# A decoder layer's state-space scan: half of the drives made by TensorE, three of four weighings on GpSimd, even and odd steps in turns

## What is computed

```python
u = conv(x) + conv_b                                   # causal, 4 taps, per channel
x_dbl = u @ xproj_w.T ; dt, Bm, Cm = split(x_dbl, 128 | 16 | 16)
delta = softplus(dt @ dtproj_w.T + dtproj_b)           # [b, token, channel]
deltaA = exp(delta[..., None] * A)                     # A = -exp(A_log): 16 states a channel
deltaBu = delta[..., None] * Bm[:, :, None, :] * u[..., None]
h = dA * h + dBu ; y = sum_n h[n] * c[n]               # for every token, in order
y = y + u * D_skip
```

## Time and profile before

| | us |
|---|---|
| median of 3 runs | 239.72 (239.43 to 240.22) |
| the profiled execution's own time | 240.53 |
| its span, first to last instruction | 238.7 |
| first scan starts | 29.98 |
| last scan ends | 168.7 |
| busy: VectorE, ScalarE, TensorE, GpSimd | 207.0, 155.1, 153.4, 151.4 |

### The profile page before, as it was taken

The page is one execution under the profiler, slowest core; times in us unless marked ns, Lnnn a source line. Parts: engine busy times, 40 slices in busy tenths (PEclk is TensorE's granted clock), DMA queues, the critical chain, the costliest instruction groups (busy, mean ns, idle before and its releaser), DMA issues.

```text
span 238.7 us, 3180 instructions
## 1 busy us (share of the span) xinstructions
PE 153.4 (64%) x804; PEld 115.0 (48%) x804; DVE 207.0 (87%) x436; ACT 155.1 (65%) x332; POOL 151.4 (63%) x166
## 2 busy tenths in 40 slices
PE   0169780987735857776495566575966776756554
PEld 0136470865724556674394545453944453533141
DVE  2297999989899899999999999999999998983841
ACT  2155889883798866857796677486357796843240
POOL 3410497498868498979888987697417354550732
PEclk9999998599795555958679997786797999995667
DMA  6992822753633445645463324310000000100003
GB/s 166 308 357 86 221 93 76 188 138 100 194 93 93 137 122 136 131 105 141 105 162 113 131 50 138 86 39 1 4 0 0 0 0 3 45 0 0 0 0 132
DMA packets 15105, 23.25 MB, mean 97 GB/s; under 512 B 1136, under 2 KB 6640, under 8 KB 15088
## 3 DMA queue, kind: packets, MB, share of 16 engines
q1 hardware_dynamic: 13792, 21.92, 33.2%
q10 hardware_dynamic: 1296, 1.15, 1.4%
HBM read 21.88 MB, written 1.18 MB: 97 GB/s over the span
## 4 chain that ended last, share of the span: by engine, by line
DVE 34%; PE 26%; issue 18%; ACT 13%; POOL 3%; DMA 2%; SPq 1%; DVEq 0%; POOLq 0%; ACTq 0%
DVE hid L1063 9%; DVE prod L1074 6%; PE pY L750 6%; PE pF L244 4%; ACT pD L484 3%; PE pA L244 3%; DVE w L1232 3%; PE pF L882 2%; POOL drive L340 2%; DMA x_sb<-x 2%; DVE am L996 2%; PE pA L714 2%; DVE hid_sb L1063 2%; PE pA L723 2%; DVE tf L1239 2%
## 5 line engine op out<-in xcount | busy, mean ns | idle before, releaser
L340 POOL TENSOR_TENSOR drive<-du,bc 128x512 f32<-128x512 f32 x64 | 79.6, 1272 | 7.9 <-DVE du L1047 2.5
L484 ACT ACTIVATE pD<-delta,negA 128x255 f32<-128x255 f32 x128 | 55.0, 468 | 17.4 <-DVE hid L1063 13.2
L1063 DVE TENSOR_TENSOR_SCAN hid<-pD,drive 128x512 f32<-128x512 f32 x48 | 58.8, 1225 | 2.7 <-ACT pD L484 0.9
L750 PE MATMUL pY<-ident,prod 128*128 128x128 f32 x256 | 45.9, 343 | 17.8 <-POOL prod L378 13.8
L750 PEld LDWEIGHTS pY<-ident,prod 128*128 128x128 f32 x256 | 40.5, 183 | 21.7 <-DVE prod L1074 12.2
L1074 DVE TENSOR_TENSOR prod<-hid,bc 128x512 f32<-128x512 f32 x48 | 32.7, 681 | 0.7 <-PE pY L750 0.3
L378 POOL TENSOR_TENSOR prod<-hid_sb,bc 128x512 f32<-128x512 f32 x16 | 20.3, 1269 | 10.6 <-DVE hid_sb L1063 9.4
L365 POOL TENSOR_TENSOR w<-w 128x352 f32<-128x352 f32 x16 | 16.6, 1041 | 14.1 <-DVE w L1232 13.8
L244 PE MATMUL pF<-ident,w 128*128 128x128 f32 x64 | 12.7, 337 | 11.4 <-ACT w L578 4.5
L1063 DVE TENSOR_TENSOR_SCAN hid_sb<-pD,drive 128x512 f32<-128x512 f32 x16 | 19.2, 1203 | 0.0
L319 POOL TENSOR_SCALAR ve<-mv 128x2 f32<-128x2 f32 x12 | 2.7, 222 | 25.3 <-DVE mv L979 25.3
(11 more groups left out here) (157 smaller groups left out, 347.3 us busy)
## 6 DMA issues: line engine op xcount, KB each, us to landing
bc<-bc_dram SPq DMA_DIRECT2D x32, 512.0 KB, 4.8
w<-w_gate_up SPq DMA_DIRECT2D x1, 1408.0 KB, 9.8
x_sb<-x SPq DMA_DIRECT2D x4, 256.0 KB, 3.8
fs_t<-w_in_t SPq DMA_DIRECT2D x1, 1024.0 KB, 12.4
out<-x_sb ACTq DMA_DIRECT2D x8, 128.0 KB, 1.8
w<-w_down SPq DMA_DIRECT2D x1, 704.0 KB, 11.1
ctx_t<-w_out_t SPq DMA_DIRECT2D x1, 512.0 KB, 12.1
xproj<-xproj_t SPq DMA_DIRECT2D x1, 160.0 KB, 3.0
```

What stands on the lines that cost most here:

```text
L340: pool.tensor_tensor(drive[:, s % 2, h], du[:, b, h].unsqueeze(1).to_broadcast([P, SPS, T]), bc[:, g % 4, 0].rearrange("p (n t) -> p n t", ...
L484: act.activation(decay[:, h, n, 1:T], delta[:, b, h, 1:T], ACT.Exp, scale=negA[:, h, k:k + 1]).then_inc(S["decay_ready"], 1)
L750: ins = pe.matmul(pY[:, j, h * P:(h + 1) * P], prod[:, s % 2, h, n, j * P:(j + 1) * P], ident[:], start=(s + n + h + j == 0), stop=False, ...
L1063: dve.tensor_tensor_scan(hid_sb[:, k % 2] if pooled(s, h) else hid, decay[:, h].rearrange("p n t -> p (n t)"), drive[:, s % 2, h].rearrang ...
```

## The change

TensorE makes the drives of the even steps. The new `turn_du` transposes du of a sequence (4 matmuls) and `out_du` copies it out to `duT` (ScalarE, 512 columns). `prep_bc` gets four small matmuls more that make B with tokens on the partitions, which `prep_bt` copies to `bT` (ScalarE, 32 columns). `diagonals_b` on ScalarE writes, for each even step, four diagonal 128x128 matrices (two token blocks, two states) from a column of `bT` and the identity. `drive_pe` then multiplies duT by these diagonals, four matmuls of 128 columns, into the second bank of `pD`. GpSimd keeps the drives of the odd steps.

The order of half steps becomes (even, h=0), (odd, h=0), (even, h=1), (odd, h=1) for each pair of steps. Even decays go to SBUF (`decay_sb`, two buffers), odd decays to the first bank of `pD` (one buffer); even drives have one buffer (second bank of `pD`), odd drives two. The freed bank is `pE`, which holds the state of (even, h=1), the one half step in four that VectorE still weighs; GpSimd weighs the other three from `hid_sb` (now four buffers). `prod` has four buffers of a half step, and `sum_step` sums a half step (4 matmuls) instead of a step.

Also: `prep_relu` moves from VectorE to ScalarE; the loads of x for sequences 1 to 3 get a semaphore each, where VectorE waited for all three; even steps load only C; all five written orders are new. In particular the six maxima over expert weights (`wmax_in`, `wmax_ctx`), which stood ahead of the first scan, now stand among the scans, and `gate_up3(0,1,0)` and `stats3(1)`, which stood before the last scan, stand behind it.

```diff
-        hid_sb = sb("hid_sb", [P, 2, SPS * T])
-        prod = sb("prod", [P, 2, H, SPS, T])
+        drive = sb("drive", [P, 2, SPS, T])
+        hid_sb = sb("hid_sb", [P, 4, SPS * T])
+        decay_sb = sb("decay_sb", [P, 2, SPS, T])
+        diag = sb("diag", [P, 2, JT, SPS, P])
+        bT = sb("bT", [P, NB, JT, NS])
+        duT = sb("duT", [P, NB, JT, D])
+        prod = sb("prod", [P, 4, SPS, T])
...
-        def count(g, h, by_pool):
-
-            return sum(pooled(u // H % STEPS, u % H) == by_pool for u in range(H * g + h))
+        def unit(b, s, h):
+
+            return H * SPS * (STEPS // 2 * b + s // 2) + 2 * h + s % 2
+
+        def of_kind(b, s, h):
+
+            return unit(b, s, h) // 2
+
+        def by_dve(q):
+
+            return q % 4 == 2
+
+        def n_dve(q):
+
+            return (q + 2) // 4
+
+        def n_pool(q):
+
...
-                    sp.wait_ge(S["drive_ready"], H * (g - 3))
-                    sp.wait_ge(S["weighed0"], count(g - 3, 0, False))
-                    sp.wait_ge(S["weighed1"], count(g - 3, 0, True))
-                rows = bc_dram[b].rearrange("(k n) t -> k n t", k=2)[:, SPS * step:SPS * (step + 1)]
-                sp.dma_start(bc[:, r].rearrange("p k (n t) -> p k n t", n=SPS), rows.partition_broadcast(P))\
+                    if g >= 5:
+                        sp.wait_ge(S["drive_ready"], H * ((g - 3) // 2))
+                    q = unit((g - 4) // STEPS, (g - 4) % STEPS, 1)
+                    sp.wait_ge(S["weighed_d"], n_dve(q))
+                    sp.wait_ge(S["weighed_p"], n_pool(q))
+                rows = bc_dram[b].rearrange("(k n) t -> k n t", k=2)[1 - step % 2:, SPS * step:SPS * (step + 1)]
...
                     pool.wait_ge(S["du_ready" if b else "du0"], b or 1)
                 pool.wait_ge(S[f"bc_load{g % 4}"], 16 * (g // 4 + 1))
-                if g >= 2:
-                    pool.wait_ge(S["scanned"], H * (g - 2) + h + 1)
-                pool.tensor_tensor(drive[:, s % 2, h], du[:, b, h].unsqueeze(1).to_broadcast([P, SPS, T]),
+                if k >= 2:
+                    pool.wait_ge(S["scanned"], 2 * (k - 2) + 2)
+                pool.tensor_tensor(drive[:, k % 2], du[:, b, h].unsqueeze(1).to_broadcast([P, SPS, T]),
...
-            drive_step(1, 7, 0); drive_step(1, 7, 1); prep_du(2); drive_step(2, 0, 0); weigh(1, 7, 1)
-            drive_step(2, 0, 1); drive_step(2, 1, 0); drive_step(2, 1, 1); drive_step(2, 2, 0); rsqrt(1, 1)
-            weigh(2, 1, 1); drive_step(2, 2, 1); drive_step(2, 3, 0); drive_step(2, 3, 1); drive_step(2, 4, 0)
-            drive_step(2, 4, 1); drive_step(2, 5, 0); weigh(2, 3, 1); smooth2(0); smooth1(1); drive_step(2, 5, 1)
-            drive_step(2, 6, 0); weigh(2, 5, 1); drive_step(2, 6, 1); prep_du(3); drive_step(2, 7, 0)
-            drive_step(2, 7, 1); drive_step(3, 0, 0); weigh(2, 7, 1); drive_step(3, 0, 1); residual2(0)
-            drive_step(3, 1, 0); drive_step(3, 1, 1); drive_step(3, 2, 0); rsqrt(2, 0); rsqrt(1, 2)
-            drive_step(3, 2, 1); drive_step(3, 3, 0); drive_step(3, 3, 1); weigh(3, 1, 1); smooth2(1)
-            drive_step(3, 4, 0); drive_step(3, 4, 1); drive_step(3, 5, 0); weigh(3, 3, 1); smooth1(2)
...
-                u = H * (STEPS * b + s) + h
-                if s == 0:
+                i = of_kind(b, s, h)
+                if s + h == 0:
                     act.wait_ge(S["delta_ready"], b + 1)
-                    act.wait_ge(S["decay_zero"], 1)
+                    act.wait_ge(S["decay_zero"], 2)
                     act.wait_ge(S["A_ready"], 1)
-                if u >= 2:
-                    act.wait_ge(S["scanned"], u - 1)
+                if s % 2:
+                    to = decay
+                    if i:
+                        act.wait_ge(S["scanned"], 2 * i)
+                else:
+                    to = decay_sb[:, i % 2]
+                    if i >= 2:
+                        act.wait_ge(S["scanned"], 2 * i - 3)
...
+            def diagonals_b(b, s):
+
+                k = of_kind(b, s, 0) // 2
+                act.wait_ge(S["bt_out"], b + 1)
+                if k >= 2:
+                    act.wait_ge(S["pe_driven"], 2 * (k - 1))
+                else:
+                    act.wait_ge(S["constants"], 4)
+                for j in range(JT):
+                    for n in range(SPS):
+                        i = SPS * s + n
+                        act.activation(diag[:, k % 2, j, n], ident[:], ACT.Copy, scale=bT[:, b, j, i:i + 1]).then_inc(S["diag_b"], 1)
+
+            def prep_bt(b):
+                act.wait_ge(S["bc_out"], b + 1)
+                act.activation(bT[:, b].rearrange("p j n -> p (j n)"), turned_bank(b)[:, T:T + JT * NS], ACT.Copy).then_inc(S["bt_out"], 1)
+
+            def out_du(b):
+                act.wait_ge(S["du_turned"], b + 1)
+                act.activation(duT[:, b].rearrange("p j d -> p (j d)"), conv_bank(b), ACT.Copy).then_inc(S["du_out"], 1)
...
+            def prep_relu(b):
+
+                act.wait_ge(S["pre_mm"], b + 1)
+                if b > 1:
+                    act.wait_ge(S["delta_ready"], b - 1)
+                for h in range(H):
+                    act.activation(z_pos[:, b % 2, h], conv_bank(b)[:, h * T:(h + 1) * T], ACT.Relu, bias=dtb[:, h:h + 1])\
+                       .then_inc(S["z_pos_ready"], 1)
+
...
+                    pe.matmul(turned_bank(b)[0:E, 0:T], xbc_t[:, h], u_t[:, b, h], start=(h == 0), stop=(h == H - 1))
+                for j in range(JT):
+                    for h in range(H):
+                        ins = pe.matmul(turned_bank(b)[:, T + j * NS:T + (j + 1) * NS], u_t[:, b, h, j * P:(j + 1) * P], xbc_t[:, h, 0:NS],
+                                        start=(h == 0), stop=(h == H - 1))
...
+            def turn_du(b):
+                pe.wait_ge(S["du_ready" if b else "du0"], b or 1)
+                for j in range(JT):
+                    for h in range(H):
+                        ins = turn(pe, conv_bank(b)[:, j * D + h * P:j * D + (h + 1) * P], du[:, b, h, j * P:(j + 1) * P])
+                ins.then_inc(S["du_turned"], 1)
+
+            def drive_pe(b, s, h):
+
+                k = of_kind(b, s, h)
+                pe.wait_ge(S["du_out"], b + 1)
+                pe.wait_ge(S["diag_b"], JT * SPS * (k // 2 + 1))
+                if k:
+                    pe.wait_ge(S["scanned"], 2 * k - 1)
+                for j in range(JT):
+                    for n in range(SPS):
+                        ins = pe.matmul(pD[:, 1, n * T + j * P:n * T + (j + 1) * P], duT[:, b, j, h * P:(h + 1) * P], diag[:, k // 2 % 2, j, n],
+                                        start=True, stop=True)
+                ins.then_inc(S["pe_driven"], 1)
...
+            def sum_step(b, s, h):
+
+                q = unit(b, s, h)
+                if by_dve(q):
+                    pe.wait_ge(S["weighed_d"], n_dve(q))
+                else:
+                    pe.wait_ge(S["weighed_p"], n_pool(q))
...
             def prep_stats(b):
-                if b == 0:
-                    dve.wait_ge(ld["x0"], 16)
-                else:
-                    dve.wait_ge(ld["x"], 16 * (NB - 1))
...
+                q, k = unit(b, s, h), of_kind(b, s, h)
+                dve.wait_ge(S["decay_ready"], SPS * (q + 1))
+                dve.wait_ge(S["drive_ready" if s % 2 else "pe_driven"], k + 1)
+                if by_dve(q):
+                    if n_dve(q) > 1:
+                        dve.wait_ge(S["weighed_d"], n_dve(q) - 1)
+                elif n_pool(q) > 4:
+                    dve.wait_ge(S["weighed_p"], n_pool(q) - 4)
+                dve.tensor_tensor_scan(pE[:] if by_dve(q) else hid_sb[:, n_pool(q) % 4],
+                                       (decay if s % 2 else decay_sb[:, k % 2]).rearrange("p n t -> p (n t)"),
+                                       drive[:, k % 2].rearrange("p n t -> p (n t)") if s % 2 else pD[:, 1],
                                        0.0, ALU.mult, ALU.add).then_inc(S["scanned"], 1)
...
+            def weigh(b, s, h):
+
+                g, q = STEPS * b + s, unit(b, s, h)
+                dve.wait_ge(S["scanned"], q + 1)
+                dve.wait_ge(S[f"bc_load{g % 4}"], 16 * (g // 4 + 1))
+                if q >= 4:
+                    dve.wait_ge(S["summed"], q - 3)
+                dve.tensor_tensor(prod[:, q % 4].rearrange("p n t -> p (n t)"), pE[:], bc[:, g % 4, 1], ALU.mult).then_inc(S["weighed_d"], 1)
...
+            max_w2(0); max_w2(1); scale_w12(); zeros(); prep_delta(0); du_first(); prep_bc(1); scan(0, 0, 0)
+            scan(0, 1, 0); scan(0, 0, 1); weigh(0, 0, 1); scan(0, 1, 1); scan(0, 2, 0); wmax_in(0); wmax_in(1)
```

344 lines of the change are left out of this document (169 added, 175 removed).

## The result

The change makes the kernel slower: 250.25 us (median of 4 runs, 249.27 to 251.46) where the kernel before has 239.92 beside it; the ratio on record is 1.0458, with a 95% interval of 1.040 to 1.0515 (the two medians alone give 1.043). I had forecast 235.7 us, a range up to 243.5, and a chance of 0.30 of any slowdown. Some executions of a kernel take over 1.5% longer than its fastest, and the ratios leave them out: two of four in experiment 12, five of twelve in experiment 11, at most two in the others. In the text, "after" is the changed kernel.

The account below looks back on a forecast made before the run. VectorE bounds the scan stage now, ScalarE after the change: first decay 26.6 + work 124.8 + idle 10 = 161.4; last scan ends 162.9, tail 71.8, span 234.7, plus 1.0 gives 235.7 us. Range 229.5 to 243.5.

Parts of the forecast that it names:

- The sums of work: Scan stage: busy time after the change of VectorE 107 us, GpSimd 114, ScalarE 124.8, TensorE 110 to 126.
- Head: Before the scans: split loads of x start the first decay about 1.6 us earlier, at 26.6; first scan about 30.5.
- Decays into SBUF: ScalarE in the scan stage: half the decays go to SBUF at an unchanged slot of 0.40 us, nothing added.
- Rival 4: ScalarE: each of 64 decays written to SBUF costs 0.03 us more, 1.9 us, time 237.6; chance 0.05.
- ScalarE is the new bound: Scan stage: ScalarE, with 124.8 us of work, 92% of the same 136 us, sets the pace.
- ScalarE's idle time: Scan stage, first to last decay: 10 us idle, 4 as the low end and 22 as the high one.
- The copies of w2: ScalarE's idle time: three copies of w2 in a row leave 2 us uncovered.
- the waits for `adq` and `dbc`: ScalarE's idle time: two chains of copy, matmul and copy in sequences 2 and 3 leave 4.5 us uncovered.
- the odd decays: ScalarE's idle time: odd decays have one buffer and wait for the odd scan before, 2 us.
- Rival 2: Scan stage: the single drive bank makes scans wait for `drive_pe`, 8 us beyond ScalarE's pace, time 243.7; chance 0.30.
- Rival 3: Last sequence: all engines loaded and an expert chain in turn, idle time 14 us, time 239.7, no change; chance 0.12.
- Rival 5: Scan stage: VectorE waits for GpSimd, as scans need a free `hid_sb`; held within the range, no chance given.
- The tail: After the last scan: 70.0 us plus 1.8 us of work moved out of the scan stage, 71.8.

Follow-up runs that it names:

- experiment 12: Changed kernel with VectorE's 16 weighings cut from 512 elements to 128, part of the computation left out: ratio 1.0319 to the kernel before.
- experiment 11: Kernel before with only the loads of x split and three pairs of relus made by ScalarE: ratio 0.9889 to the kernel before.
- 3: Changed kernel with only the first two of 16 groups of diagonals of B, the others left out: ratio 1.043 to the kernel before.
- 2: Changed kernel with each of the 128 drive matmuls replaced by a transpose, factor B left out: ratio 1.0492 to the kernel before.
- 10: Changed kernel with GpSimd's 48 weighings cut to half their elements, 256 instead of 512: ratio 1.0175 to the kernel before.
- experiment 1: Changed kernel with a ring of eight slots instead of four for the loaded rows of B and C: ratio 1.0269 to the kernel before.
- 16: Changed kernel with eight load and six product slots, plus three places of the written orders changed, work kept: ratio 1.0147 to the kernel before, 241.61 us.
- 14: Changed kernel with eight load and six product slots, most diagonals out, transposes for drive matmuls, GpSimd's weighings halved, VectorE's quartered: ratio 0.9895 to the kernel before.
- experiment 5: Changed kernel with eight slots for loaded rows and six instead of four for weighed products: ratio 1.0322 to the kernel before.
- 17: Kernel with eight load slots, six product slots and three moved places, plus six more moves in ScalarE's and TensorE's orders: ratio 1.0189 to the kernel before.
- experiment 4: Changed kernel with two banks for TensorE's drives, the scan that VectorE weighs writing to SBUF: ratio 1.0692 to the kernel before.
- experiment 9: Changed kernel with eight load slots, odd decays also to SBUF, both halves of pD as drive banks: ratio 1.0704 to the kernel before.
- 7: Changed kernel with each engine's remaining work behind its last stage step in the order of the kernel before: ratio 1.0502 to the kernel before.

## Why the prediction was wrong

**The sums of work came out, except VectorE's.** ScalarE 123.45 us where I had 124.8, GpSimd 109.25 (114), TensorE 111.14 (110 to 126) at a granted clock of 0.95 (above 0.8). VectorE has 115.35 where I had 107. I took 31 us off for the weighings; their rows went from 32.0 to 10.3 us in the stage, 21.7 less, and the scans' rows stayed (78.0 and 77.6). I had counted scans at a distance of 1.14 us, but a scan that stands alone costs its 1.21 to 1.22. TensorE's sum was luck: I priced its drives from transposes at 0.15 us each, they cost 0.26 and 36.6 us in all, and the sums of weighed states, which I had left alone, fell from 45.9 to 36.2 us at the higher clock. (With the upper price my own sum was 126, not "still below ScalarE's" 124.8.)

**Head: right.** First decay forecast 26.6, measured 26.61; with split loads alone it starts at 25.55, so the 2.7 us less 1 of the sum are both there. First scan forecast 30.5, measured 30.85. Against split loads alone (27.17) the way over turn, copy and drive costs 3.7 us. I wrote that this costs nothing; that rested on ScalarE being the bound, and nothing here shows it.

**Decays into SBUF: right.** Their rows are longer (498 against 469 ns), their distance is 0.40 as before; here ScalarE in after:

```profile
35.20 0.90 ACT L508 ACTIVATE decay_sb<-delta,negA 128x255 f32<-128x255 f32 x2
36.00 0.62 ACT L483 ACTIVATE z_ln<-z_abs 128x512 f32<-128x512 f32 x1
```

Two in 0.80 us. The Trainium skill ("ScalarE: Activation LUTs", "Step-by-step: what each stage is for") has PSUM as the faster target; the trace agrees for the length of one, not for the time that many take. Rival 4 is out.

**"ScalarE is the new bound": the step that failed.** I took the engine with the largest sum and asked how near to 100% it runs. Last decay end forecast 161.4, last scan end 162.9; measured 170.9 and 172.2, 9.3 us later. ScalarE's idle time was 21.4 us, not 10, at the upper bound of 22 that I had worked out and then left outside the range. The copies of w2 waited 2.3 us in all (forecast 2) and the waits for `adq` and `dbc` came to 4.2 (4.5); the term that was furthest off is the odd decays, 7.8 us of waiting for scans where I had 2, because the scans themselves came late. But the size is not the point: 16.4 us less work on ScalarE changed nothing that could be measured (3). Nor was it TensorE's sum (2) or GpSimd's alone, of which 26 us are worth 6.7 (10). And no mean over the stage could say it: ScalarE is 98% busy in the first sequence, 89% in the second, 79% and 74% after that, and I worked with one number for all four.

**What took its place.** Four engines at 76 to 85%, each in a fixed order, tied by rings of one to four slots: a late step holds back scans by a few us, and there are many places. This picture is argued from the waits. Shown are its parts: the ring of loads, 4 us (1); the written order in three places, 4 to 5 us (16); and that work is not all of it, since all cuts together give no more than their sum and leave 21 us of VectorE idle (14). Before, VectorE was the one full engine and 5.5 us of idle time was all that it lost to such places, and the others had 25 to 46 us of slack each. Now each engine idles for 21 to 34 us of the stage, and none is always busy, so that a late step of one is no longer hidden behind the work of another. With both repairs, 1 (with 5) and 16, the kernel stands at 1.0147: some 7.5 us of the slowdown are gone, 3.5 are left, and the gain that I had forecast is not there. What holds the rest is open. In the first two sequences it is neither ScalarE's work alone (3) nor the six moved places (17), while all cuts together shorten them by 7.3 us (14).

**Rival 2** had the right sign and, with 243.7, the nearest time; my range ended just below it, at 243.5, although I had given it 0.30. Its mechanism does not show as the cause: scans waited 3.3 us for `drive_pe` (2.5 of them in the rows above), far below the 10 that I had set for it, and with a second bank they still waited 3.3 (4). But both runs with a second bank (4, 9) paid for it elsewhere, so what the single bank costs in time was not measured.

**Rival 3** named "the last sequence"; the fourth takes 39.8 us before and after. An expert chain among the scans did cost time as it said, but that of sequence 0 in the third (16); the rest of the loss is in the tail.

**Rival 5**, GpSimd, I had let into the range with no time of its own; the loads that wait for its weighings are the 4 us of experiment 1. I had not asked what waits for a weighing that GpSimd now makes late: SP's load four steps on, and behind it the odd drive.

**The tail.** Forecast 71.8, measured 75.1. I priced what moved on VectorE (1.8 us; its busy time rose by 2.5) and not what moved on GpSimd, 6.7 us more busy time. With before's order the tail does not shrink (7), nor does it when the stage ends 12 us earlier (76.4 in 14). Which wait makes up the rest was not tried.

## What to carry to other kernels

Adding up each engine's work gives a lower bound. It described this stage while one engine was 96% busy, and not when four stood at 76 to 85%. When a change levels in-order engines like that, price every wait as if nothing hid it, stretch by stretch, and follow each buffer to the load that refills it; here the idle time came out at the upper bound. Before such a rebalance is given up or kept, its written order has to be made for it: three moved places were worth 4 us here, 16 us of work on the engine with the largest sum next to nothing. Small parts that only take work from the full engine (loads split by semaphore, relus on ScalarE) are worth trying alone.

## What the runs showed of the hardware

Two inputs in SBUF cost VectorE and GpSimd both: a scan of 512 columns took 1670 ns on the mean instead of 1210 (experiment 9), a weighing 952 instead of 687 (experiment 4), while GpSimd's 1273 ns became 1322 (VectorE's 16 weighings changed) and 1518 (its 32 odd scans). It is no fixed price: single scans with both inputs in SBUF took 1.19 to 2.23 us in experiment 9. The one at 57.26 us began 0.16 us ahead of a weighing on GpSimd and took 1.20, and GpSimd's next two weighings took 3.35 us, where two of its operations take 2.50 undisturbed (at 26.07 us in after); the one at 44.45 us began behind a weighing and took 2.14. One input in PSUM was enough to avoid it (1203 ns in the same kernel). The Trainium skill, "SBUF — State Buffer", section "Who interferes with whom", says that a VectorE instruction with two SBUF inputs contends with a GpSimd instruction that reads SBUF; the traces agree, and add the sizes.

TensorE's clock fell for single stretches although it worked for three quarters of the stage. In experiment 5 the granted clock was 0.50 (1.2 GHz) in the stretch from 104.5 to 106.6 us, and eight drive records took 2.05 us where they take 1.06 at full clock (2.4 GHz). Before it fell, the engine had made only transposes from 99.87 to 103.2 us, with two waits of 0.67 us between them, and had then waited 1.35 us. The table by stretch (as above), then TensorE in order of time:

```profile
104.50:106.60 2.10, 2.07 (x10) 2.10 (x11) 0.00 (x0) 2.10 (x8) 2.10 (x3) 0.50 0.05 17
```

```profile
104.53 2.05 PE L832 MATMUL pD<-diag,duT 128*128 128x128 f32 x8 [1.35 <-DVE hid_sb L1164]
```
